# A graph network in one program: where four small pieces of work and four weight loads stand

## The reference, cut to what matters

```
# first expert layer, one expert of eight per node (x after a layer norm)
H = gelu(xf @ W1 + b1)                         # 256 -> 1024
probs = softmax(H @ Wg + bg)                   # 8 logits per node
assign = argmax(probs)
for e in range(8):
    y = H @ Wd[e] + bd[e]                      # 1024 -> 256
    out += where(assign == e, probs[:, e] * y, 0)

# relational layer, 8 relations, 8 heads of 32 features (x after a layer norm)
h_all = einsum('nf,rof->rno', x, W)            # per relation a 256x256 weight
h_src, h_dst = h_all[edge_type, src], h_all[edge_type, dst]
scores = sum(h_src * attn_src) + sum(h_dst * attn_dst)
w = softmax over the edges of each dst of leaky_relu(scores)
out = segment_sum(h_src * w)
```

## Time and profile before

| | us |
|---|---|
| runs shown, median of 3 (lowest to highest) | 5295.25 (5291.57 to 5301.25) |
| the profiled execution | 5306.25 |
| its span, first to last instruction | 5304.5 |
| PE, DVE, POOL, ACT busy in the span | 4224.0, 3158.7, 2119.3, 1855.4 |

### The profile page before, as it was taken

How to read it: one execution, slowest core, us unless ns; L and a number is a source line. 1 busy time by engine, 2 the same in 40 slices (tenths; PEclk the granted TensorE clock), 3 DMA queues, 4 the chain that set the end, 5 groups by cost and what they waited for, 6 DMA issues and landing times. The chain is left out here.

```text
span 5304.5 us, 100541 instructions
## 1 busy us (share of the span) xinstructions
PE 4224.0 (80%) x21913; PEld 3177.1 (60%) x21914; DVE 3158.7 (60%) x8451; ACT 1855.4 (35%) x5244; POOL 2119.3 (40%) x2259
## 2 busy tenths in 40 slices
PE   0877777777778798079989997887787767999999
PEld 0545555555554797068874445565555547878877
DVE  3469999989988443100002216777777775555555
ACT  0244444444443232022223335444444422222222
POOL 2266556556553112600002217777777741111110
PEclk9988899989998898589999997888888888999999
DMA  2466556556553210320114444444334320000000
GB/s 78 142 191 170 164 167 169 167 162 170 167 165 95 103 40 25 99 98 32 34 68 158 178 171 114 111 112 110 107 107 107 107 86 21 16 14 14 16 14 11
DMA packets 231520, 540.71 MB, mean 102 GB/s; under 512 B 46641, under 2 KB 129087, under 8 KB 222559
## 3 DMA queue, kind: packets, MB, share of 16 engines
q0 software_dynamic: 112976, 348.83, 23.8%
q1 hardware_dynamic: 118287, 189.45, 10.1%
HBM read 422.56 MB, written 115.55 MB: 101 GB/s over the span
## 5 line engine op out<-in xcount | busy, mean ns | idle before, releaser
L441 POOL DMA_INDIRECT attn_KV<-kv_tab,attn_stage x832 | 833.7, 1002 | 545.7 <-PE attn_SP L556 294.3
L1782 POOL DMA_INDIRECT rel_V<-h_tab,rel_stage x832 | 853.9, 1026 | 318.1 <-issue 195.3
L556 PE MATMUL attn_SP<-attn_KV 128*128 128x264 f32 x1664 | 581.4, 447 | 289.9 <-DVE node L658 287.2
L1882 PE MATMUL rel_SP<-rel_V,rel_OH 128*128 128x264 f32 x1664 | 569.0, 460 | 97.8 <-DVE node L1953 89.0
L556 PEld LDWEIGHTS attn_SP<-attn_KV 128*128 128x128 f32 x1664 | 291.1, 207 | 513.3 <-issue 492.4
L543 PE MATMUL attn_QP<-node,attn_OHT 128*128 x1664 | 494.1, 430 | 17.9 <-ACT attn_OHT L458 9.0
L2156 ACT ACTIVATE moe_HT<-moe_HB,moe_b 128x128 f32<-128x128 f32 x800 | 228.0, 368 | 674.0 <-PE moe_HB L2173 674.0
L1882 PEld LDWEIGHTS rel_SP<-rel_V,rel_OH 128*128 128x128 f32 x1664 | 311.7, 215 | 228.1 <-DVE node L1953 171.5
L658 DVE SCALAR_TENSOR_TENSOR node<-node,same,attn_SP 128x264 f32 x832 | 395.3, 475 | 64.8 <-DVE attn_carry L701 30.7
L2173 PE MATMUL moe_HB<-moe_YT,moe_W 128*128 128x128 f32 x3200 | 412.5, 284 | 0.0
L1953 DVE TENSOR_TENSOR node<-node,rel_SP 128x264 f32 x832 | 349.2, 420 | 105.4 <-PE rel_SP L1882 45.1
(11 more groups left out here) (336 smaller groups left out, 7052.8 us busy)
## 6 DMA issues: line engine op xcount, KB each, us to landing
h_tab<-pr_H SPq DMA_DIRECT2D x50, 1056.0 KB, 3.9
attn_KV<-kv_tab,attn_stage POOLq DMA_INDIRECT x832, 3.6
rel_V<-h_tab,rel_stage POOLq DMA_INDIRECT x832
kv_tab<-qkv_KV SPq DMA_DIRECT2D x50, 256.0 KB, 2.0
attn_runs<-runs SPq DMA_DIRECT2D x52, 192.0 KB
rel_runs<-runs SPq DMA_DIRECT2D x52, 192.0 KB
exp_Wd<-in_wd SPq DMA_DIRECT2D x8, 1024.0 KB
y_sorted<-gate_zeros SPq DMA_DIRECT2D x8, 928.0 KB
```

Source lines behind the costliest of these rows:

```text
L441: pool.indirect_dma_start(out=KV[:, i * IT + u, 0:2 * FEAT], out_offset=None, in_=d["kv_tab"][:, :], in_offset=bass.IndirectOffsetOnAxis(a ...
L556: pe.matmul(SP[u % SUMS][:, 0:NUMC], KV[:, j * IT + u, 0:P], KV[:, j * IT + u, FEAT:ROW], start=True, stop=True).then_inc(s["sums"], 1)
L1782: pool.indirect_dma_start(out=V[:, i * IT + u, :], out_offset=None, in_=d["h_tab"][:, :], in_offset=bass.IndirectOffsetOnAxis(ap=stage[:, ...
L1882: pe.matmul(SP[(j + u) % SUMS][:, 0:NUMC], OH[:, j * IT + u, :], V[:, j * IT + u, :], start=True, stop=True).then_inc(s["sums"], 1)
```

## The change

It has six parts.

1. `relmask` is written by one DVE instruction with two broadcast inputs in place of eight.
2. The maximum, the subtraction and the power of the logits are done tile by tile inside the loop of `attend_and_route`: a reduce and a subtraction on DVE, and on POOL a power of 128x8 (was one of 128x400 in the sort phase).
3. The loads of W1, b1, Wd and WN and the attention vectors are issued at the start of the sort phase, and the fold is done in it; its PE part stands ahead of the two counting matmuls.
4. The loads of bd (to all 128 partitions) and WX are issued in the scatter phase, behind the first five tile loads.
5. In the expert phase the bias matmul is gone; DVE adds the bias in place of the copy and reads the expert's number itself. Neither the expert phase nor the relation phase has loads or a fold at its start.
6. `relmask` is read back at the start of the relational layer, ahead of the other loads on SP, and DVE waits for it after it has cleared `node`.

```
-            for r in range(RELS):
-                link(dve.tensor_scalar(tm[:, :, r], typf[:, 0:SPAD], float(r), None, ALU.is_equal))
+            link(dve.tensor_tensor(tm, typf[:, 0:SPAD].unsqueeze(2).to_broadcast([P, SPAD, RELS]),
+                                   m.iota_f[:, 0:RELS].unsqueeze(1).to_broadcast([P, SPAD, RELS]), ALU.is_equal))
...
# attend_and_route, POOL
-                pipeline(pool, lambda t, i: front_scale(pool, m, f, t + 4, i), LEAD, 1, BLOCKS)
+                def body(t, i):
+                    front_scale(pool, m, f, t + 4, i)
+                    n, j = t - 1, (i + 1) % 2
+                    if has(n, BLOCKS):
+                        pool.wait_ge(s["shifted"], t)
+                        pool.tensor_tensor(m.ex[:, bass.ds(n * EXPERTS, EXPERTS)], m.e_const[:, :], LS[:, j, :], ALU.pow
+                                           ).then_inc(s["powed"], 1)
...
# attend_and_route, DVE
-                        dve.tensor_tensor(m.logits[:, bass.ds((t - 1) * EXPERTS, EXPERTS)], LG[:, 0:EXPERTS],
-                                          bg[:, :], ALU.add).then_inc(s["logits"], 1)
+                        need(dve, s["shifted"], t - 1)
+                        dve.tensor_tensor(logits[:, :], LG[:, 0:EXPERTS], bg[:, :], ALU.add).then_inc(s["logits"], 1)
                     front_copy(dve, dve.tensor_copy, f, t + 2, i, s["hidden"], 2)
+                    if has(t - 1, BLOCKS):
+                        dve.wait_ge(s["logits"], t)
+                        dve.tensor_reduce(most[:, :], logits[:, :], AX.X, ALU.max).then_inc(s["most"], 1)
...
                         dve.tensor_copy(OT[:, j, :], TO[:, 0:FEAT]).then_inc(s["oT"], 1)
+                    if has(t - 1, BLOCKS):
+                        dve.wait_ge(s["most"], t)
+                        need(dve, s["powed"], t - 2)
+                        dve.tensor_scalar(LS[:, j, :], logits[:, :], most[:, 0:1], None, ALU.subtract).then_inc(s["shifted"], 1)
...
# sort_by_expert, SP
+                sp.dma_start(heads[:, :], d["att"][:, :]).then_inc(s["a"], 16)
+                for k in range(2):
+                    sp.dma_start(WN[:, k, :], d["wr_n"][k * P:(k + 1) * P, :]).then_inc(s["wn"], 16)
+                for k in range(2):
+                    sp.dma_start(m.W1[:, k, :], d["w1"][k * P:(k + 1) * P, :]).then_inc(s["w"], 16)
+                sp.dma_start(m.b1[:, :], d["b1"][:, :]).then_inc(s["w"], 16)
+                for k in range(KC):
+                    sp.dma_start(m.Wd[:, k, :], d["wd"][k * P:(k + 1) * P, :]).then_inc(s["w"], 16)
+                sp.wait_ge(s["w"], 16 * (3 + KC))
# POOL
-                pool.wait_ge(s["shifted"], 1)
-                pool.tensor_tensor(grid(ex), per_expert(m.e_const), grid(m.logits), ALU.pow).then_inc(s["powed"], 1)
# PE
+                pe.wait_ge(s["wn"], 32)
+                pe.wait_ge(s["heads"], 4)
+                for h in range(2):
+                    for r in range(RELS):
+                        for k in range(2):
+                            mm = pe.matmul(fold(h, r), WN[:, k, r * FEAT + h * P:r * FEAT + (h + 1) * P], AB[:, k, :],
+                                           start=(k == 0), stop=(k == 1))
+                    mm.then_inc(s["fold"], 1)
                 pe.wait_ge(s["chosen"], 1)
# DVE
-                link(dve.tensor_reduce(top[:, :], grid(m.logits), AX.X, ALU.max))
-                dve.tensor_tensor(grid(m.logits), grid(m.logits), per_row(top), ALU.subtract).then_inc(s["shifted"], 1)
...
-                dve.wait_ge(s["powed"], 1)
+                dve.wait_ge(s["a"], 16)
+                for k in range(2):
+                    for j in range(2):
+                        dve.tensor_scalar(AB[:, k, j * HEADS:(j + 1) * HEADS], ...).then_inc(s["heads"], 1)
...
+                dve.wait_ge(s["fold"], 2)
+                for h in range(2):
+                    for j in range(2):
+                        dve.tensor_copy(m.WX[:, h, at:at + RH]..., SP_[h]...).then_inc(s["folded"], 1)
...
# scatter_rows, SP, behind the first five tile loads
+                sp.dma_start(m.bd[:, :], d["bd"][0:1, :].to_broadcast([P, EXPERTS * FEAT])).then_inc(s["w"], 16)
+                for k in range(2):
+                    sp.dma_start(m.WX[:, k, 0:RELS * FEAT], d["wr_t"][k * P:(k + 1) * P, :]).then_inc(s["w"], 16)
...
# expert_of_sorted, PE and DVE (and the loads and the waits for s["w"] are gone)
-                        pe.matmul(RB[j][:, 0:FEAT], m.ones_row[0:1, :], bd[0:1, bass.ds(e * FEAT, FEAT)],
-                                  start=True, stop=False)
...
+                        e = dve.value_load(m.tile_expert[0:1, bass.ds(t - 1, 1)], min_val=0, max_val=EXPERTS - 1)
...
-                        dve.tensor_copy(R[:, j, :], RB[j][:, 0:FEAT]).then_inc(s["out"], 1)
+                        dve.tensor_tensor(R[:, j, :], RB[j][:, 0:FEAT], bd[:, bass.ds(e * FEAT, FEAT)], ALU.add).then_inc(s["out"], 1)
...
# project_relations: the loads, the four AB steps, the fold and the four copies are gone
...
# relational_layer, SP and DVE
+                sp.dma_start(rel_of[:, :], d["relmask"][:, :]).then_inc(s["rel_of"], 16)
                 sp.wait_ge(s["cleared"], 1)
...
                 dve.wait_ge(s["cleared"], 1)
+                dve.wait_ge(s["rel_of"], 16)
```

117 lines of the change are left out of this document (50 added, 67 removed).

## The result

| | us |
|---|---|
| before, median of 4 runs | 5293.41 (5289.8 to 5301.25) |
| changed, median of 4 runs | 5149.77 (5145.27 to 5156.78) |
| ratio, with its 95% interval | 0.9728 (0.9716 to 0.974) |
| profiled execution: before, changed | 5306.25, 5156.78 |

The kernel is 143.6 us faster. Forecast were 5156 and -139.4 us. The spans of the two profiled executions differ by 149.3 us, and the following table says where. A phase is counted from its first instruction to that of the next; differences are taken before rounding.

The account below looks back on a forecast made before the run. No one engine bounds the kernel: PE's list sets the gate and expert loops, single waits the stretches between. Terms -9.4 + 2.2 - 47.8 + 4.5 - 24.5 - 36.0 - 28.4 = -139.4 give 5156 us from the median; range 5128 to 5196.

Parts of the forecast that it names:

- Masks: Relation masks: one instruction takes 7.2 us in place of eight taking 16.59, -9.4 us (bounds 0 and -10).
- The bound of 16.3 us: Relation masks: the new instruction keeps 2.4 ns a column and gains 0.
- Gate loop: Turn stays 6.61 us, small power 1.7 (bounds 1.3 and 4.4); bare chain behind the last tile +2.2 us.
- the slow rival D: Gate loop: the small power on POOL isn't cheap and sets the turn; at 10 us a power, 5360 us; chance 0.03.
- The rival of the lock: Gate loop: POOL and DVE block each other, the turn grows by 0.05 us, +2.5, 5159 us; chance 0.08.
- Sort: Sort phase: 38.6 us in place of 86.4, -47.8 us, PE's fold ending last before the counting (bounds -41 and -54.7).
- rival B: Sort and scatter: loads don't hide; at 276 GB/s sort gains -41, scatter costs +10; 5168 us, chance 0.12.
- Scatter: Scatter phase: the sixth tile load lands behind the 3.1 MB of bd and WX, +4.5 us once (bounds 0 and +10).
- Start of the expert phase, relation phase: First transpose 2.4 us into the expert phase, -24.5 us; relation phase without loads and fold at its start, -28.4.
- Expert loop: Without the bias matmul each of 58 tiles loses 0.62 us, -36.0 us (bounds -16.8 and -44).
- rival A: Expert loop: the 0.33 us gap belongs to the first matmul with a register operand and stays; 5175 us, chance 0.14.
- the forecast's own sign: Whole kernel: the forecast is wrong if any phase the change doesn't touch moves by more than 10 us.

Follow-up runs that it names:

- e4_fold_behind_counting: The changed kernel with PE's two counting matmuls ahead of the fold in the sort phase, on the slower chip: 5530.26 us, ratio 0.971.

## Why the prediction was right, point by point

**Masks.** One instruction of 7.22 us for the forecast 7.2. (The working's own numbers, 1.05 ns a column and 0.15, give 7.28.) The bound of 16.3 us, for a rate that belongs to the type, is excluded.

**Gate loop.** Right: turn unchanged, PE 250.00 of 250.00 us, and +2.2 in the rows of the bare chain; the phase's own +1.9 is too near to chance to say so. The small power takes 1.64 alone and 1.8 in the loop; 1.7 was forecast. It could have been read: the forecast says that no power of this width is in the trace, but the last layer of the kernel before has 50 of them, here with the least, the median and the longest in ns:

```profile
L2139 POOL TENSOR_TENSOR moe_ex<-e_const,moe_L x50: 1636/1647/1648, 4392.3 to 5274.9; 128x8 f32<-128x8 f32 x50
```

So neither the bound of 4.4 us nor the one thing said for the slow rival D had a ground. The rival of the lock falls, with L1133 inside a power. Its rule in the Trainium skill, "SBUF — State Buffer", section "Who interferes with whom", foretells that one of the two stands still for the other's whole instruction. The trace shows a part of it at most: POOL lost up to 0.25 us where DVE's two-input instruction had begun just ahead of it, and DVE, lost nothing inside a power and 0.08 where one began just behind it. At the start of the long power in the sort it lost more: L1184 took 1.08 us, and the same instruction takes 0.29 in the changed kernel, without a power beside it. What holds it there stays open, but it isn't the end of the power. The rival on the slow side has the right mechanism and the wrong size: POOL begins to rule between three and four powers a tile, and we have one.

**Sort.** The order of the waits was right: WN, fold, counting, DVE's chain. Forecast were 38.6 us to DVE's last copy, and it ends at 38.4 (2085.47 to 2123.82), at the granted clock of 0.50; the phase of 39.1 holds the barrier too. That the fold's place cost about 8 us was shown by moving it: 6.6. The loads were in by 32.5 us there, so they are hidden under the 39.1, and rival B falls in the sort; in the scatter the measured 6.4 to 7.2 lie between its +10 and the +4.5 of the forecast.

**Scatter.** One gap at the sixth tile, as forecast, but 6.4 us (7.2 against the second profile) in place of 4.5, and by another way. The forecast issued the sixth load about 4 us into the phase and had it wait behind 7.4 us of transfer. It was issued at 10.8 us, as the scatter that frees its slot landed late although it goes through POOL's own queue, and WX landed 13.3 us behind bd's issue (2126.84 to 2140.14). With the loads moved away the gap is gone.

**Start of the expert phase, relation phase.** -24.8 for -24.5, and -28.4 for -28.4. These were waits on a path with nothing beside them, and there the reading of a start and an end is exact. No run takes these two, or the masks, back by themselves: they rest on the two profiles of the kernel before against those with the change.

**Expert loop.** This is the term that was mis-sized: "0.62 us a tile, 0.29 for the two weight loads and 0.33 in which PE waited for nothing shown" measured 0.82 us, 47.3 in the 58 tiles in place of 36.0, beyond the term's lower bound of -44 too. The forecast took the start of the bias as the point to which the list would move up. But ahead of the bias there was a second, unmarked gap of 0.20 us, though the forecast says under rival A that the bias had none ahead: the bias stood 3.77 to 3.78 us behind the first weight load of the hidden layer, and Wd now stands 3.57 behind it. The forecast's own lower bound had this turn in it, with a slip: 16 x 0.21 + 34 x 0.114 is 7.24 us and not 7.3, which makes -48. The list without gaps was the right reading, and it was taken for an extreme. The three bias experiments put it down to the one-row matmul: 128 rows cost 0.43 us a turn for the same 256 columns, one row 0.82 with or without a register address. The Trainium skill, "TensorEngine Tiling (Array Packing)", section "Tiling Modes", says that a change of the tiling mode drains the engine; the trace agrees, if the one-row matmul runs in another mode, which no row shows. I hadn't weighed that rule. The rival that the gap stays fell, too. That one row is the cause is shown; by what mechanism it is so, is not.

**What I left out, and luck.** The terms of the sum measured -150.1 us together against the first profile of the kernel before and -145.4 against the second, for -139.4 forecast; the expert loop alone gave 11.3 more than forecast. The relational layer, put at nothing, gave back 9.5 or 11.2, about 6.7 over all profiles, and stretches that the change doesn't touch took 8.7 or 2.9 more away. That the medians differ by 143.6, only 4.2 from the forecast, is so in part luck: a gain that was put too small and a loss that was left out lay against each other. By the forecast's own sign, a phase that the change doesn't touch and that moves by more than 10 us, the relational layer was at the edge. But the sign was too narrow: the attention moves by up to 23 us among profiles in which nothing of it is changed.

## What to carry to other kernels

A matmul of one row between matmuls of 128 costs more than its own slots, ahead of it and behind it: here 0.39 us of 0.82; give it all rows or put the sum on another engine that is idle. What a wait hides is free room: the loads and the fold would have fitted under the old power as well, and when work is moved into such room, it belongs behind what the next engine is waiting for. When a group leaves a list, measure from the last thing ahead of it to the first behind it, by the step of the groups, and not from its own start. A queue of its own doesn't keep small transfers clear of large ones: the median scatter landed 7.1 us behind its issue beside 3.1 MB of loads, and 2.7 in the kernel before.

## What the runs showed of the hardware that was not expected

- Two chips differ by 7.7% on one program: the kernel before took 5699.71 us on one and about 5294 on the others. Of the 374 us between two profiles of kernels with the change (`e4_fold_behind_counting` and the changed kernel) 288 lie in the relational layer, 40 in the attention, 40 in the stretch ahead of its first matmul (233 us against 194) and 11 in the scatter. All four have gathers or scatters by rows in them. The expert loop took the same (474.4 us with the one-row bias on both).
- A power on GpSimd takes 0.161 us a column at 400 columns and 1.64 us at 8, 1.61 in a row; up to 0.25 more where VectorE's instruction with two inputs in SBUF began just ahead of it, and none where the power began first.
- Over 950 us of the relational layer the granted clock is 0.86 to 0.88 in the eight profiles with the change on chips of this speed, and 0.89 in both without it; no edit there explains it.
